# Roots by logarithm and exponential, and the attention residual on ACT and POOL, in a top-k kernel

## The reference

```python
h = tok(x)                                   # frames @ DCT
h = h + attn(layernorm(h))                   # softmax(x x^T) x, per clip
h = h + ffn(layernorm(h), Wq, bq, ln_g, ln_b, keys0, keys1, down, up)

def layernorm(x): return (x - mean(x)) / sqrt(var(x) + 1e-5)
def ffn(x, ...):
    q = (x @ Wq.T + bq) in 8 heads of 64
    q = (q - mean) / sqrt(var + 1e-5) * ln_g + ln_b
    s0, s1 = l2norm(q[:32]) . l2norm(keys0), l2norm(q[32:]) . l2norm(keys1)
    top 16 of each; top 16 of their 256 sums; w = softmax
    out = sum over picked experts of gelu(x . down[i]) * w * up[i]
```

## Time and profile before

| | before |
|---|---|
| median of three executions | 2025.39 us (2025.3 to 2026.98) |
| the profiled execution | 2031.43 us, span 2029.6 us |
| mean granted PE clock | 0.812 of full |
| DVE busy | 95% of the span |
| PE, POOL, ACT busy | 80%, 71%, 61% |

### The profile page before, as it was taken

The page is one execution under the profiler, slowest core; times in us unless marked ns, Lnnn a source line. Parts: engine busy times, 40 slices in busy tenths (PEclk is TensorE's granted clock), DMA queues, the critical chain, the costliest instruction groups (busy, mean ns, idle before and its releaser), DMA issues.

```text
span 2029.6 us, 47236 instructions
## 1 busy us (share of the span) xinstructions
PE 1632.5 (80%) x11023; PEld 1169.5 (58%) x11023; DVE 1919.0 (95%) x15718; ACT 1232.0 (61%) x3883; POOL 1433.2 (71%) x2561
## 2 busy tenths in 40 slices
PE   5577888788888888888888788888878888986667
PEld 3235566566656655665666556656656565655456
DVE  2499999999999999999999999999999999999992
ACT  3346666666666666566556766656675665665554
POOL 2247777686777767777776777777687777767775
PEclk8877888888888787888888787888888888788765
DMA  1000000000000000000000000000000000000000
GB/s 44 7 10 4 19 7 13 13 7 19 7 19 9 13 13 6 19 7 19 7 6 22 6 19 7 19 7 7 19 9 20 7 19 7 6 13 9 7 6 11
DMA packets 46669, 24.87 MB, mean 12 GB/s; under 512 B 4827, under 2 KB 46116, under 8 KB 46390
## 3 DMA queue, kind: packets, MB, share of 16 engines
q1 hardware_dynamic: 46390, 21.85, 3.9%
HBM read 11.58 MB, written 10.26 MB: 11 GB/s over the span
## 4 chain that ended last, share of the span: by engine, by line
DVE 79%; PE 11%; ACT 5%; issue 4%; POOL 1%; SPq 1%; DMA 0%; DVEq 0%; ACTq 0%
DVE idx L1071 11%; DVE idx L1078 11%; DVE hrest L1065 10%; DVE alpha L1039 10%; DVE vals L1069 7%; DVE vals L1062 7%; DVE c L1109 5%; DVE crest L1103 5%; DVE top L1106 3%; DVE top L1100 3%; PE QB L526 2%; DVE beta L1044 2%; PE FB L418 1%; PE QB L514 1%; DVE lo L1033 1%
## 5 line engine op out<-in xcount | busy, mean ns | idle before, releaser
L914 POOL TENSOR_TENSOR bw<-beta,wp 128x1024 bf16<-128x1024 bf16 x240 | 505.2, 2135 | 347.3 <-issue 171.6
L526 PE MATMUL QB<-bw,alpha 128*128 128x48 bf16 x5120 | 554.5, 277 | 106.7 <-issue 101.1
L526 PEld LDWEIGHTS QB<-bw,alpha 128*128 128x128 bf16 x5120 | 521.0, 150 | 149.2 <-issue 139.4
L749 ACT ACTIVATE WD<-QB 32x96 f32<-32x96 f32 x1280 | 307.6, 240 | 84.5 <-PE QB L526 71.6
L1039 DVE TENSOR_SCALAR alpha<-hi 128x1024 bf16<-128x1024 bf16 x640 | 274.9, 502 | 0.0
L475 PE MATMUL SC<-WK,hidT 128*128 128x512 f32 x320 | 241.0, 846 | 12.6 <-issue 11.8
L1071 DVE FIND_INDEX8 idx<-vals,sraw 128x8 uint32<-128x64 f32 x1280 | 250.6, 218 | 0.0
L1078 DVE FIND_INDEX8 idx<-vals,hrest 128x8 uint32<-128x64 f32 x1280 | 250.6, 219 | 0.0
L1065 DVE MATCH_REPLACE8 hrest<-vals,sraw 128x64 f32<-128x64 f32 x1280 | 249.6, 207 | 0.0
L1062 DVE MAX8 vals<-sraw 128x8 f32<-128x64 f32 x1280 | 169.1, 207 | 14.1 <-ACT sraw L729 14.1
L1069 DVE MAX8 vals<-hrest 128x8 f32<-128x64 f32 x1280 | 166.6, 208 | 0.0
(11 more groups left out here) (206 smaller groups left out, 3583.3 us busy)
## 6 DMA issues: line engine op xcount, KB each, us to landing
res<-h_scratch SPq DMA_DIRECT2D x80, 64.0 KB, 1.9
xin<-in_x SPq DMA_DIRECT2D x32, 128.0 KB
h_scratch<-h2n SPq DMA_DIRECT2D x32, 128.0 KB
out<-ofin SPq DMA_DIRECT2D x64, 64.0 KB, 1.5
h_scratch<-h2n SPq DMA_DIRECT2D x32, 28.5 KB
out<-ofin SPq DMA_DIRECT2D x16, 57.0 KB
xin<-in_x SPq DMA_DIRECT2D x32, 28.0 KB
xin<-in_x SPq DMA_DIRECT2D x32, 0.2 KB
```

Source lines behind the costliest of these rows:

```text
L526: last = mm(bank[:, 48 * u:48 * u + 48], alpha[:, buf, a, :, 8 * p + u], bwv[:, :, a, :, 8 * p + u], start=(a == 0), stop=(a == 1))
L749: last = A(WD[r, RING[(t - 4) % NT], :, 8 * p:8 * p + 8], blocks[r, :, :, g], ACT.Copy)
L914: last = tt(bw[:, buf, NY * i:NY * i + NY, :], beta[:, buf, :, :], wp[:, buf, i, :].unsqueeze(1).to_broadcast([128, NY, 256]), ALU.mult)
```

## The change

The bit guess and `seed` are gone. ACT makes a near guess as exp(-0.5 ln(c x)), two instructions (`guess`, `row_guess`), and POOL makes one step of four operations (`step`) in place of twelve. ACT also makes `sv`, which was DVE's. At (1, 3) DVE is left with the two reciprocals; ACT copies O times `rden` to the new tile `osc`, and POOL adds `hcs` to it, two instructions for each clip. The copies to `hcs` at (0, 0) move behind the root. The roots of v3 and n2 stand on ACT at (3, 3) and in phase 3 of tile 0; the key root in phase (0, 3) of the start.

```diff
@@ ACT
+            def guess(p, x_, scale, bias, sem_, value):
+                A(p, x_, ACT.Ln, scale=scale, bias=bias).then_inc(sem_, 1)
+                act.wait_ge(sem_, value)
+                A(p, p, ACT.Exp, scale=-0.5).then_inc(sem_, 1)
+            def row_guess(i, j):
...
+                guess(sxh[i][:], ss[i][:], (2.0 * D) ** (2.0 / 3.0) / D, cmin[:, 1:2], sem_, 3 * j + 1)
+                A(sv[i][:], ss[i][:], ACT.Identity, bias=cmin[:, 0:1]).then_inc(sem_, 1)
@@ ACT, front (0, 0), between the squares and the copies to hcs
+                    row_guess(0, j)
@@ ACT, front (1, 3)
+                    for b in range(2):
+                        bank = f_wait(act, f"O{b}", j)
+                        act.wait_ge(s["rden_full"], 2 * j + b + 1)
...
+                        for c, (st, n) in enumerate(CH):
+                            last = A(osc[0:n, b, c, :], bank[0:n, 129 * c:129 * c + D], ACT.Copy,
+                                     scale=rden[0:n, 3 * b + c:3 * b + c + 1])
+                        last.then_inc(s["osc_full"], 1)
@@ ACT, front (2, 0), between the squares and h2n
+                    row_guess(1, j)
@@ ACT, front (3, 3)
+                    act.wait_ge(s["v3_full"], j + 1)
+                    guess(xh3[:], v3[:], 2.0 ** (2.0 / 3.0), 0.0, s["guess3"], 2 * j + 1)
@@ ACT, slot, ahead of the waits for QB and of ofin
+                if p == 3 and t == 0 and exists(k, 0, 0):
+                    act.wait_ge(s["n2_steps"], 2 * k + 2)
+                    guess(xh4[:], n2[:], 2.0 ** (2.0 / 3.0), 0.0, s["guess4"], 2 * k + 1)
@@ POOL
+            def step(out_, x_, p, a, lead, sem_, base):
+                tt(a, p, p, ALU.mult).then_inc(sem_, 1)
...
+                tt(a, a, x_, ALU.mult).then_inc(sem_, 1)
...
+                tt(a, lead, a, ALU.subtract).then_inc(sem_, 1)
...
+                tt(out_, p, a, ALU.mult).then_inc(sem_, 1)
@@ POOL, front (1, 3)
+                        tt(h2c[:, b, 0:2, :], osc[:, b, 0:2, :], hcs[:, b, 0:2, 0:D], ALU.add)
+                        tt(h2c[0:n, b, 2, :], osc[0:n, b, 2, :], hcs[0:n, b, 2, 0:D], ALU.add).then_inc(s["h2c_full"], 1)
@@ DVE, front (1, 3)
-                        for c, (st, n) in enumerate(CH):
-                            last = V.scalar_tensor_tensor(out=h2c[0:n, b, c, :], in0=bank[0:n, 129 * c:129 * c + D],
-                                                          scalar=rden[0:n, 3 * b + c:3 * b + c + 1], in1=hcs[0:n, b, c, 0:D],
-                                                          op0=ALU.mult, op1=ALU.add)
-                        last.then_inc(s["h2c_full"], 1)
@@ DVE
-                seed(v3[:], xh3[:], y3[:], s["seed3_full"])
-                seed(n2[:], xh4[:], y4[:], s["seed4_full"])
-                                row_seed(0, k + 1, s["seed1_full"])
-                    row_seed(1, j, s["seed2_full"])
```

More of the change, by code:

```diff
@@ L105, in build @@
         cdig = sb("cdig", [128, NS])
[L106 removed]
+        clead = sb("clead", [128, 80])
+        crow = sb("crow", [128, 6])
+        cmin = sb("cmin", [128, 2])
         WcT = sb("WcT", [128, 512])
@@ L135, in build @@
         h2c = sb("h2c", [128, 2, 3, D])
+        osc = sb("osc", [128, 2, 3, D])
         h2n = sb("h2n", [128, 2, 3, D])
@@ L640, in front @@
                         A(E[0:n, b, c, :], bank[0:n, 0:NF], ACT.Exp, bias=cneg64[0:n, :]).then_inc(s["e_full"], 1)
+                if (t, p) == (1, 3):
+                    for b in range(2):
+                        bank = f_wait(act, f"O{b}", j)
+                        act.wait_ge(s["rden_full"], 2 * j + b + 1)
+                        after(act, s["h2_full"], 2 * j + b - 1)
+                        for c, (st, n) in enumerate(CH):
+                            last = A(osc[0:n, b, c, :], bank[0:n, 129 * c:129 * c + D], ACT.Copy,
+                                     scale=rden[0:n, 3 * b + c:3 * b + c + 1])
+                        last.then_inc(s["osc_full"], 1)
                 if (t, p) == (2, 0):
@@ L771, in _ @@
             tt = nc.gpsimd.tensor_tensor
[L773 to L781, removed]
+            def step(out_, x_, p, a, lead, sem_, base):
+                tt(a, p, p, ALU.mult).then_inc(sem_, 1)
+                pool.wait_ge(sem_, base + 1)
+                tt(a, a, x_, ALU.mult).then_inc(sem_, 1)
+                pool.wait_ge(sem_, base + 2)
+                tt(a, lead, a, ALU.subtract).then_inc(sem_, 1)
+                pool.wait_ge(sem_, base + 3)
+                tt(out_, p, a, ALU.mult).then_inc(sem_, 1)
             def setup():
@@ L801, in late @@
             def late(t, p):
[L802 to L804 removed]
+                if (t, p) == (0, 3):
+                    pool.wait_ge(s["kss_part"], 3)
+                    pool.wait_ge(s["kguess"], 2)
+                    step(ky[:], kss[:], kxh[:], ka[:], clead[0:64, 0:2], s["knewton"], 0)
             def front(j, t, p):
                 if (t, p) == (0, 2):
[L808 to L809 removed]
+                    pool.wait_ge(s["guess1"], 3 * j + 3)
+                    step(sy[0][:], sv[0][:], sxh[0][:], sa[:, 0:6], crow[:], s["newton1"], 4 * j)
+                if (t, p) == (1, 3):
+                    for b in range(2):
+                        pool.wait_ge(s["osc_full"], 2 * j + b + 1)
+                        pool.wait_ge(s["hcs_full"], 2 * j + b + 1)
+                        tt(h2c[:, b, 0:2, :], osc[:, b, 0:2, :], hcs[:, b, 0:2, 0:D], ALU.add)
+                        n = CH[2][1]
+                        tt(h2c[0:n, b, 2, :], osc[0:n, b, 2, :], hcs[0:n, b, 2, 0:D], ALU.add).then_inc(s["h2c_full"], 1)
                 if (t, p) == (2, 0):
[L811 to L812 removed]
+                    pool.wait_ge(s["guess2"], 3 * j + 3)
+                    step(sy[1][:], sv[1][:], sxh[1][:], sa[:, 0:6], crow[:], s["newton2"], 4 * j)
                 if (t, p) == (3, 3):
[L814 to L816 removed]
+                    pool.wait_ge(s["v3_full"], j + 1)
+                    pool.wait_ge(s["guess3"], 2 * j + 2)
+                    step(y3[:], v3[:], xh3[:], sa[:], clead[:, 0:40], s["newton3"], 4 * j)
+                    pool.wait_ge(s["newton3"], 4 * j + 4)
                     tt(std[:], v3[:], y3[:], ALU.mult).then_inc(s["std_steps"], 1)
@@ L975, in setup @@
                                     ALU.mult).then_inc(s["kn_full"], 1)
-            def row_seed(i, j, done):
-                dve.wait_ge((s["ss1_full"], s["ss2_full"])[i], 2 * j + 2)
-                V.tensor_scalar(sv[i][:], ss[i][:], 1.0 / D, 1e-5, ALU.mult, ALU.add).then_inc((s["sv1"], s["sv2"])[i], 1)
-                dve.wait_ge((s["sv1"], s["sv2"])[i], j + 1)
-                seed(sv[i][:], sxh[i][:], sy[i][:], done)
             def front(j, t, p):
-                if (t, p) == (0, 1) and j == 0:
-                    row_seed(0, j, s["seed1_full"])
                 if (t, p) == (1, 3):
@@ L989, in front @@
                         bank = f_wait(dve, f"O{b}", j)
-                        dve.wait_ge(s["hcs_full"], 2 * j + b + 1)
+                        after(dve, s["h2c_full"], 2 * j + b - 1)
                         V.reciprocal(rden[:, 3 * b:3 * b + 2], bank[:, 128:258:129])
```

52 lines of the change are left out of this document (26 added, 26 removed).

## The result

The changed kernel takes 2140.89 us (median of four, 2137.24 to 2142.8). The kernel before, measured beside it, takes 2026.18 (2025.3 to 2028.4). The ratio is 1.0562, 95% interval 1.0544 to 1.0581. One of the four executions of one kernel further down (no loads at n2, 2185.55 us at a granted clock of 0.71, the others at 0.80) is a slow one and is left out of its time. The profiled execution of the changed kernel has a span of 2139.9 us and a mean granted clock of 0.798.

The account below looks back on a forecast made before the run. A chain of ACT and PE was to become the bound: 116.1 + 10.2 = 126.3 us a pair against 119.5, +6.8, plus 0.7 for the clock; over 14 pairs 105, so 2025.4 + 105 = 2130 us, range 2050 to 2190.

Parts of the forecast that it names:

- The bound after the change: The chain of ACT and PE passes DVE's 115.5 us a pair; DVE idles 90 us or more for ACT's `zexp`.
- The period: Each of 14 loaded pairs grows by 6.8 us from the chain plus 0.7 for the clock: 7.5, ends 1.7 and 11.
- the head: Start of the kernel, two row roots and the root of v3: taken as 0, with ends -5 and +8.
- (a): `osc` on ACT ahead of `zexp` of tile 2: full price, 1.85 us a pair.
- (b): Second row root on ACT, ahead of a `wp` in tile 2 that PE waits for: full price, 3.2 us.
- (c): Root of v3 on ACT ahead of `zexp` of tile 4: 3.0 less the `stdT` wait of 1.05, 1.95 us.
- (d): First row root on ACT, ahead of `wp` of tile 0 that PE waits for: full price, 3.2 us.
- (e): Root of n2 on ACT ahead of `ofin` in tile 0: 3.0 us, hidden in ACT's waits for PE; otherwise 3 more.
- The room, 3.4 us a pair: PE's idle time for `bw` in tiles 1 and 0, taken as the chain's room: 119.5 - 3.4 = 116.1 us a pair.
- Where DVE stands: DVE stalls before L1088: 5.3 us in tile 3, where `zexp` had 1.8 of room; also tiles 4, 0 and 1.
- The clock: PE's lower granted clock adds 0.7 us a pair, 0 to 3.6; rival: 3.6 gives 2171, with (e) unhidden 2210; 10%.
- Every switch costs more than its row: Rival: each of six switches on the chain costs its load's 1.28 us again, 7.7 a pair: 2238 us; 6%.

Follow-up runs that it names:

- no loads at n2: Changed kernel with the logarithm of the root of n2 replaced by a plain copy, so its two table loads go: 2146.3 us, ratio 1.0575.
- roots only: Changed kernel with `h2c` formed by DVE as before, so that only the roots are changed: 2126.6 us, ratio 1.0497.
- loads alone: Kernel before with two table loads added at each of the places (b) to (e), seeds, Newton and `h2c` as before: 2128.8 us, ratio 1.0500.
- one table set: Changed kernel with the set holding both Ln and Exp loaded, 33 loads instead of 163: 2009.4 us, ratio 0.9914 to before.
- one set and `h2c` on DVE: Changed kernel with one table set for Ln and Exp and `h2c` formed on DVE again: 1966.3 us, ratio 0.9706 to before.
- row root 1 later: Changed kernel with the first row root moved behind the second `wp` and its WD in tile 0: 2172.7 us, ratio 1.0725 to before.

## Why the prediction was right, point by point

*The bound after the change.* Right. DVE's idle time was forecast at 90 us or more ahead of `zs`, ended by `zexp`; it is 172.8. DVE is busy for 1854.7 us (forecast 1850), ACT for 1450.7 (1470), and the table loads number 163 of 1283 ns. DVE's own work is 127.5 - 12.6 = 114.9 us a pair (115.5). PE's idle time for `bw` is gone from tiles 0 and 1 of the 14 loaded pairs, as forecast, where it was 3.4 us a pair; the 53.2 us that are left stand behind the last loaded pair and, with 0.8 us a pair, in tile 2.

*The period.* 7.5 us a pair were forecast, 8.0 came, in 14 pairs; the head gave the 0 that was taken.

*(a) `osc`, 1.85.* Over-sized: 1.3 by roots only (1.0 by the medians). It takes 1.5 to `zexp` as timed above.

*(b), (c), (d), 3.2, 1.95 and 3.2.* The places are right, and the loads are what is paid for: without them 8.3 us a pair go. (c) came out at 1.9 for its loads alone, where 1.95 was forecast for the whole root and 1.55 expected for its loads; since DVE's own work moved with it, that it is so near is not shown to be the forecast's mechanism. ACT's wait ahead of `stdT`, set against it with 1.05, is gone as forecast (22.7 us in 16 times before, 4.1 in one now).

*(e), hidden.* Right, but only behind (d), as the kernels without the loads of (d) and with a later (d) showed.

*The room, 3.4 us a pair.* This step failed, and the sum hid it. A wait of PE in tiles 0 and 1 was read as room of the whole pair. The path that sets the end runs on DVE in one stretch and on PE and ACT in the next, and room in one stretch is of no use to what is added in another. For (b) the room was 1.0 us on average. The prediction had read this very place, 1.8 us between `zexp` and `zs` in tile 3, in one of the three pairs that have most there, and then used PE's 3.4 for the sum. Reckoned for the loads alone the 3.4 made the expectation 56 us too low; with 1.1 in its place some 32 of these are explained. Of the rest, 11 to 16 lie with (c) and (e), as said above, and 4.5 in the head, where tile 5 begins at 185.74 instead of 181.25.

In the sum for the change two errors met. With 1.1 in the place of 3.4 it gives 10.2 - 1.1 + 0.7 = 9.8 us a pair and about 2163, still within the range, but 22 us above what was measured. It was set off by terms that were too large: `osc` by 0.6, and 0.6 us of Ln and Exp for each of three roots, priced on ACT, which did not show in the period (roots only and loads alone have 126.2 both). So that 2130 came within 11 us of 2140.9 is in part luck. In roots only DVE has no seeds and POOL four operations for twelve, which shortens the same path; that this is the reason is argued from there, and was not tried apart.

*Where DVE stands.* Forecast 5.3 us in tile 3 and the rest in tiles 4, 0 and 1. It is 8.1 in tile 3, 1.3 in tile 4 by (c), 1.8 in tile 1 by (d), and in tile 0 nearly nothing: 0.07 us in 12 of the 14 pairs. The smaller room, 1.0 instead of 1.8, is 0.8 of the extra in tile 3. The rest is argued: the stall is what DVE is ahead of the slower chain over the whole pair, and it is taken where that chain is next met.

*The clock, 0.7 us.* Nine pairs took 126.3 to 126.8 us, five 128.6 to 129.9, which makes a mean of 1.2 above the quickest. The one shown above has a granted clock of 0.83, a pair of 129.9 us one of 0.80 (tile 0: 0.78 against 0.72). It is of the size that was allowed for (0.7, up to 3.6); which comes first, the clock or the idle time, stays open. The far end of that rival, 2171 with 3.6 us a pair, was also given with (e) unhidden, as 2210; the sum is 2213.

*Every switch costs more than its row.* Disproved. The earlier trace rows showed 1283 ns and no gap, and in the rows of tile 2 above a load begins 0.02 us or less behind the instruction ahead of it, and the next one begins 0.01 us behind the load. The 8.3 us a pair that one table set took away are 7.7 us of loads and 0.6, and two loads in the kernel before made it slower by 1.7 us a pair, less than their own 2.57. The Trainium skill, "ScalarE: Activation LUTs", section "What ACT_TABLE_LOAD costs", has 2.66 us for a switch with its drain; by it six would be 16 us, and the measurement decides against it for this kernel.

## What to carry to other kernels

Room belongs to a place, not to a pair: read it at the next instruction at which the engine that you delay meets the one that sets the pace, behind the place of the edit (here `zexp` to `zs`, 1.1 us). Before two functions are used in turn on ACT, count the table loads in the built order: an Ln and an Exp of 6 columns took 0.5 us here and their loads 2.57. With one set that holds both, the same roots turned from 5.0% slower to 2.9% faster. And an operation taken off the busiest engine brought nothing where that engine next waited for its result.

## What the runs showed of the hardware

DVE and POOL hold each other up. The first operation of the root's step on POOL, 128 x 6, took 1468 ns on average in the changed kernel and 198 in the one with one set and `h2c` on DVE. (A POOL span is rough in the profile, but this is seven times as long.) One instance, in tile 2 of the changed kernel, with what DVE did at the time:

```profile
1141.17 2.77 DVE L1060 TENSOR_SCALAR alpha<-hi 128x1024 bf16<-128x1024 bf16 x8
1141.44 3.10 POOL L810 TENSOR_TENSOR sa<-sxh 128x6 f32<-128x6 f32 x1 [3.98 <-ACT sv L610]
1143.84 0.64 DVE L1065 TENSOR_SCALAR beta<-lo 128x256 bf16<-128x256 bf16 x4
...
1144.62 0.20 POOL L812 TENSOR_TENSOR sa<-sa,sv 128x6 f32<-128x6 f32 x1
```

It ends at 1144.54, with the last of DVE's twelve bf16 `TENSOR_SCALAR` (1144.48), and its successor takes 0.20. The same place in the kernel without the loads of (b), where the step is over before `alpha` begins, and POOL goes on to its larger products:

```profile
369.43 5.71 DVE L1060 TENSOR_SCALAR alpha<-hi 128x1024 bf16<-128x1024 bf16 x8
369.65 1.09 POOL L950 TENSOR_TENSOR wz<-wexp,rz 128x432 f32<-128x432 f32 x1
370.81 1.43 POOL L955 TENSOR_TENSOR Yw<-wz,m 128x432 f32<-128x432 f32 x1
372.20 1.31 POOL L956 TENSOR_TENSOR Ye<-ci,m 128x432 bf16<-128x432 f32 x1
```

Now DVE's eight take 5.71 us instead of 2.77. In the loaded pairs of the changed kernel the eight take 2.77 us in tiles 0 to 3, where nothing of POOL's stands beside them but the root's small step in tile 2, and 5.53 on average in tile 4, where they overlap with POOL's for 3.5 us. Before it was 4.99 in tile 4 and 3.92 in tile 1. Which engine is held up turns on small shifts between the two queues: without the loads of (c) DVE's eight take 2.81 us in tile 4, and there it is a product of POOL's that takes long, 4.57 us in the row below where the changed kernel has 1.37 at 1195.79:

```profile
1176.28 4.57 POOL L955 TENSOR_TENSOR Yw<-wz,m 128x432 f32<-128x432 f32 x1
```

Over a whole run the 640 `alpha` instructions were busy for 227.0 us in the kernel without the loads of (c), 249.6 with one set and `h2c` on DVE, 264.8 in the changed kernel, 274.9 in the kernel before and 303.8 without the loads of (b). So the time of DVE's own work moves by up to 77 us with what POOL does beside it, which no sum by the row of one instruction shows. The Trainium skill, "SBUF — State Buffer", section "SBUF: two separate sides", describes such a thing: VectorE and GpSimd share one pair of ports, a VectorE instruction in a fast two-port mode needs it alone, and whichever comes second is blocked. The traces agree in that one holds the other up. They differ in when it gets in: the page has the pair held for one instruction, and in tile 2 of the changed kernel POOL's small operation got in only behind twelve of DVE's, not behind the first. Which mode DVE was in no run here shows.

Of POOL's 1368 us, 33 more than the 1335 that the prediction's terms give, some 40 are this (32 operations, 1.27 us more each). What the 3.10 us cost in time is open: PE has no wait behind them until tile 3.

PE's busy time is no fixed quantity either. The same 11,023 products took 1592.1 us at a mean granted clock of 0.828 (one set, `h2c` on DVE), 1617.8 at 0.798 and 1674.3 at 0.784 (row root 1 later). The kernel before is off that line, with 1632.5 at 0.812, so the mean clock alone does not give it.
